# A selective scan on VectorE, with half of its C product handed to GpSimd and one intermediate kept in PSUM

## The reference, cut to what matters

```python
A = -jnp.exp(A_log)
dA = jnp.exp(jnp.einsum('bld,dn->bldn', dt, A))
dBx = jnp.einsum('bld,bln,bld->bldn', dt, B, x)

def step(h, inp):
    dA_t, dBx_t, C_t = inp
    h = dA_t * h + dBx_t
    y_t = jnp.einsum('bdn,bn->bd', h, C_t)
    return (h, y_t)
...
return y + x * D
```

## Time and profile before

| | us |
|---|---|
| Median of 3 runs (lowest, highest) | 1213.88 (1211.88, 1214.82) |
| Profiled execution, its own time | 1216.69 |
| Its span in the profile | 1214.9 |
| From the first B product (340.29) to the end of the last accumulation (495.90) | 155.61 |

### The profile page before, as it was taken

One profiled execution on the slowest core, in us unless ns is written; L12 is line 12 of the kernel. 1 busy time (PEld: TensorE's weight loads), 2 busy tenths in 40 slices (PEclk: granted clock), 3 DMA queues, 4 the chain that ended last, 5 costly groups with the idle time before them and its releaser, 6 DMA issues.

```text
span 1214.9 us, 15485 instructions
## 1 busy us (share of the span) xinstructions
PE 1015.3 (84%) x5192; PEld 644.1 (53%) x5202; DVE 836.2 (69%) x1392; ACT 619.5 (51%) x1493; POOL 494.6 (41%) x374
## 2 busy tenths in 40 slices
PE   5999879464646666358899999999999999999998
PEld 3777654223212222136667677777767565555554
DVE  4568639977699999767888877778787445332232
ACT  2445646066477663157778777687766223211111
POOL 0022277151056671137777765677654422100000
PEclk9878859778768787679999999999999999999999
DMA  9501130300100000000000014200003000000000
GB/s 334 243 1 51 69 139 0 125 32 5 24 0 1 0 0 0 2 1 1 2 1 2 1 45 126 70 2 1 2 1 122 1 1 1 1 18 1 1 1 18
DMA packets 24319, 43.78 MB, mean 36 GB/s; under 512 B 3616, under 2 KB 19936, under 8 KB 22624
## 3 DMA queue, kind: packets, MB, share of 16 engines
q1 hardware_dynamic: 24240, 42.79, 10.5%
HBM read 41.74 MB, written 1.05 MB: 35 GB/s over the span
## 4 chain that ended last, share of the span: by engine, by line
PE 58%; DVE 24%; ACT 10%; issue 5%; POOL 1%; DMA 1%; SPq 0%; DVEq 0%; ACTq 0%; POOLq 0%
PE ps L2165 12%; PE ps L2186 8%; DVE arena L982 6%; PE ps L1723 4%; PE ps L1736 4%; PE ps L1682 3%; DVE arena L978 3%; ACT arena L1027 3%; ACT ps L2011 3%; PE ps L1707 3%; PE ps L1690 3%; PE ps L437 2%; PE ps L400 2%; PE ps L1715 2%; PE ps L1697 2%
## 5 line engine op out<-in xcount | busy, mean ns | idle before, releaser
L2204 DVE TENSOR_TENSOR arena<-arena,ps 128x512 f32<-128x512 f32 (+1 forms) x56 | 38.5, 687 | 146.0 <-ACT arena L2197 143.9
L2089 POOL TENSOR_TENSOR arena<-arena 128x4 f32<-128x4 f32 x96 | 99.0, 1032 | 47.3 <-DVE arena L1839 44.5
L2197 ACT ACTIVATE arena<-ps,arena 128x512 f32<-128x512 f32 (+1 forms) x56 | 38.4, 686 | 156.0 <-PE ps L2165 156.0
L1061 PE MATMUL ps<-arena,ident 128*128 128x512 f32 x128 | 82.6, 781 | 37.6 <-DVE arena L987 37.6
L2186 PE MATMUL ps<-wide,arena 128*128 128x256 f32 (+1 forms) x448 | 106.3, 380 | 0.0
L2011 ACT ACTIVATE ps<-ps,arena 128x128 f32<-128x128 f32 x256 | 88.4, 355 | 28.3 <-DVE arena L1818 28.3
L2003 ACT ACTIVATE arena<-ps,arena 128x512 f32<-128x512 f32 x96 | 68.1, 784 | 65.9 <-PE ps L1697 65.8
L2186 PEld LDWEIGHTS ps<-wide,arena 128*128 128x128 f32 (+1 forms) x448 | 84.7, 190 | 17.9 <-issue 1.8
L2165 PE MATMUL ps<-XT,wide 128*128 128x512 f16 (+1 forms) x384 | 93.3, 379 | 0.0
L1818 DVE TENSOR_REDUCE arena<-ps 128x4 f32<-128x512 f32 x64 | 43.8, 690 | 47.5 <-PE ps L1707 47.4
L1690 PE MATMUL ps<-wide,arena 128*128 128x512 f16 x256 | 66.6, 397 | 11.2 <-POOL arena L2069 9.1
(11 more groups left out here) (322 smaller groups left out, 2469.1 us busy)
## 6 DMA issues: line engine op xcount, KB each, us to landing
side<-in_wproj SPq DMA_DIRECT2D x1, 4096.0 KB, 14.2
wide<-in_w_down SPq DMA_DIRECT2D x1, 3584.0 KB, 13.9
side<-in_w_gate SPq DMA_DIRECT2D x1, 3520.0 KB, 30.8
side<-in_w_up SPq DMA_DIRECT2D x1, 3520.0 KB, 12.1
wide<-in_w_gate SPq DMA_DIRECT2D x2, 1728.0 KB, 11.9
side<-in_w_up SPq DMA_DIRECT2D x3, 1024.0 KB, 9.3
arena<-in_taps SPq DMA_DIRECT2D x1, 2048.0 KB, 13.6
wide<-in_wq SPq DMA_DIRECT2D x1, 2048.0 KB, 10.7
```

Of the source, the lines that this page charges most:

```text
L1061: last = pe.matmul(ps[:, 4 + 2 * c + j, :], k.ident[:, :], read[i % 2][:, 512 * j:512 * j + 512], start=(n == 0), stop=(n == NST - 1), ski ...
L2089: pool.tensor_tensor(rs[:, j, :], var[:, j, :], minus_half[:, j, :], ALU.pow).then_inc(rs_ready, 1)
```

## The change

The two halves are treated differently. For the upper half (c = 1) the B product is written back over B in PSUM banks 0 and 1, and the scan reads it there. The SBUF space of the second `dBx` buffer becomes `c_copy`. ACT copies C from PSUM into it once per pair, and POOL makes the C product of the lower half (c = 0) from `state[0]` and `c_copy`. DVE makes only the C product of the upper half. The waits follow: `read_ready` is split in two; B of the next n is spread only after the upper scan (it reads bank 0), C only after ACT's copy and DVE's C product. Three semaphores elsewhere are merged or dropped.

```diff
-    dBx = [A.take([N]) for _ in range(2)]
+    dBx, c_copy = A.take([N]), A.take([N])
...
@@ vector
             wait(dve, state_ready, i - 1)
-            dve.tensor_tensor(dBx[i % 2], dtx[:, c, :], banks(0), ALU.mult).then_inc(dBx_ready, 1)
+            product = banks(0) if c else dBx
+            dve.tensor_tensor(product, dtx[:, c, :], banks(0), ALU.mult).then_inc(dBx_ready, 1)
             dve.wait_ge(dBx_ready, i + 1)
             dve.wait_ge(dA_ready, i + 1)
-            wait(dve, read_ready, i - 1)
-            dve.tensor_tensor_scan(state[i % 2], dA[i % 2], dBx[i % 2], 0.0, ALU.mult,
-                                   ALU.add).then_inc(state_ready, 1)
-            dve.wait_ge(state_ready, i + 1)
-            dve.wait_ge(c_psum, n + 1)
-            wait(dve, summed, i - 1)
-            dve.tensor_tensor(read[i % 2], state[i % 2], banks(2), ALU.mult).then_inc(read_ready, 1)
+            wait(dve, read1_ready if c else read0_ready, n)
+            dve.tensor_tensor_scan(state[c], dA[c], product, 0.0, ALU.mult, ALU.add).then_inc(state_ready, 1)
+            if c:
+                dve.wait_ge(state_ready, i + 1)
+                dve.wait_ge(c_taken, n + 1)
+                wait(dve, summed, i - 1)
+                dve.tensor_tensor(read[1], state[1], banks(2), ALU.mult).then_inc(read1_ready, 1)
@@ scalar, at the end of each step, behind split_scalar
+            if c:
+                act.wait_ge(c_psum, n + 1)
+                wait(act, read0_ready, n)
+                act.copy(c_copy, banks(2)).then_inc(c_taken, 1)
@@ tensor, accumulate(i)
-            pe.wait_ge(read_ready, i + 1)
+            pe.wait_ge(read1_ready if c else read0_ready, n + 1)
@@ tensor, the loop (spread no longer waits itself)
             accumulate(2 * n)
             if n + 1 < NST:
-                spread(n + 1, b_parts, 0, b_psum, dBx_ready)
-                spread(n + 1, c_parts, 2, c_psum, read_ready)
+                pe.wait_ge(state_ready, 2 * n + 2)
+                spread(n + 1, b_parts, 0, b_psum)
+                pe.wait_ge(read1_ready, n + 1)
+                pe.wait_ge(c_taken, n + 1)
+                spread(n + 1, c_parts, 2, c_psum)
             accumulate(2 * n + 1)
@@ gpsimd
-        for i in range(len(w.chunks)):
-            w.split_pool(pool, i, unsplit[i % 2])
+        for i, (n, c) in enumerate(STEPS):
+            if i < len(w.chunks):
+                w.split_pool(pool, i, unsplit[i % 2])
+            if c == 0:
+                pool.wait_ge(c_taken, n + 1)
+                pool.wait_ge(state_ready, i + 1)
+                wait(pool, summed, i - 1)
+                pool.tensor_tensor(read[0], state[0], c_copy, ALU.mult).then_inc(read0_ready, 1)
```

More of the change, by code:

```diff
@@ L920, in scan @@
     state_ready = k.sem("sc_state_ready")
-    read_ready = k.sem("sc_read_ready")
+    c_taken = k.sem("sc_c_taken")
+    read0_ready = k.sem("sc_read0_ready")
+    read1_ready = k.sem("sc_read1_ready")
     summed = k.sem("sc_summed")
@@ L1048, in tensor, with spread @@
             last.then_inc(dt_psum, 1)
-        def spread(n, rows, bank, done, free):
-            wait(pe, free, KC * n)
+        def spread(n, rows, bank, done):
             for j in range(2):
@@ L1066, in tensor @@
         pe.wait_ge(parts_ready, 1)
-        spread(0, b_parts, 0, b_psum, dBx_ready)
+        spread(0, b_parts, 0, b_psum)
         pe.wait_ge(parts_ready, 2)
@@ L1070, in tensor @@
         pe.wait_ge(dt_relu, 2)
-        spread(0, c_parts, 2, c_psum, read_ready)
+        spread(0, c_parts, 2, c_psum)
         for n in range(NST):
@@ L1391, in load_whole @@
         sp.dma_start(self.k.side[:, 0:KC * FM].rearrange("p (c n) -> p c n", c=KC),
-                     self.k.a["w_up1" if up else "w_gate1"].rearrange("(c p) n -> p c n", p=P)).then_inc(self.whole_loaded, 16)
+                     self.k.a["w_up1" if up else "w_gate1"].rearrange("(c p) n -> p c n", p=P)).then_inc(self.gate_loaded, 16)
     def square(self, act, i):
-        act.wait_ge(self.whole_loaded, 16 * (i // 4 + 1))
+        act.wait_ge(self.gate_loaded, 16 * (i // 4 + 1))
         wait(act, self.squared, i)
@@ L1411, in scale @@
         if v == 0:
-            dve.wait_ge(self.gate_loaded, 80)
+            dve.wait_ge(self.gate_loaded, 32 + 80)
         if v == 5:
@@ L1598, in cross @@
     lnT_psum = k.sem("xa_lnT_psum")
-    x_scales = k.sem("xa_x_scales")
     var_done = k.sem("xa_var_done")
@@ L1624, in cross @@
     w_used = k.sem("xa_w_used")
-    out_psum = k.sem("xa_out_psum")
     added = k.sem("xa_added")
@@ L1805, in vector @@
         dve.tensor_tensor(x_w, in_inv, ln_w.unsqueeze(2).broadcast_to([P, KC, 4]), ALU.mult)
-        dve.tensor_tensor(x_b, in_inv, ln_b.unsqueeze(2).broadcast_to([P, KC, 4]), ALU.mult).then_inc(x_scales, 1)
+        dve.tensor_tensor(x_b, in_inv, ln_b.unsqueeze(2).broadcast_to([P, KC, 4]), ALU.mult).then_inc(consts, 1)
         def quantise_x(b):
@@ L2019, in take_pT @@
             act.copy(flat(pT[t]), ps[:, 4 + t, :]).then_inc(pT_ready, 1)
-        act.wait_ge(x_scales, 1)
+        act.wait_ge(consts, 1)
         take_x(0)
-        act.wait_ge(consts, 1)
+        act.wait_ge(consts, 2)
         k.norm_scalar(act, 7, range(1, B))
@@ L2095, in gpsimd @@
         round_x(0)
-        pool.wait_ge(consts, 1)
+        pool.wait_ge(consts, 2)
         for j in range(3):
```

1 line of the change is left out of this document (removed).

## The result

The changed kernel takes 1223.02 us in the median of 4 runs (1221.21 to 1224.87), the one before 1214.12 (1211.88 to 1214.82). The ratio is 1.0069, with a 95% interval of 1.0044 to 1.0095: slower by about 8.9 us (5.3 to 11.5 by the interval), where 5.9 were forecast. The profiled execution took 1221.21. Further down, one of the ten runs of e4_warm (1284.89 us) and one of the six of e8_spread (3378.49 us) fell in a slower state, and the ratios leave them out.

The account below looks back on a forecast made before the run. Before, DVE bound at 9.42 us a pair (141.3); after, POOL and PE: 12 x 10.12 + 3 x 8.94 = 148.3, +7.0 less 1.1 = +5.9, on the median 1213.88 giving 1219.8 us, range 1205 to 1227.

Parts of the forecast that it names:

- DVE: One of two C products leaves DVE: 1.14 us less per pair, 8.28 a pair, 18.2 us if nothing else bound.
- POOL's product: POOL's C product of 1024 columns takes 2.36 us, between bounds of 2.12 and 2.56.
- in-place product: DVE's upper B product written into PSUM costs nothing extra; upper bound twice 1.21, costing 2.7 us in all.
- scan from PSUM: The upper scan's input from PSUM adds no time.
- Loop 1: Lower scan, POOL's product and two subtractions exclude each other at the SBUF port: 8.94 us a pair, upper scan exempt.
- Loop 2: Lower scan, POOL's product, PE's accumulation and B's spread, DVE's B product: 8.46 us a pair at high clock, 10.12 at low.
- How often the clock is low: PE's lower accumulation starts at the low clock in 12 of 15 intervals, after longer idle stretches.
- The end: Behind the last lower scan one C product is gone: -1.14 us.
- ACT's copy, the merged semaphores, the start: ACT's 1.01 us copy is hidden, merged semaphores add no wait, and the first pair starts as before.
- The clock up all through: Rival: PE's part is 2.42 us in nearly all pairs, loop 1 binds, -8.3 us, 1205.6; chance 0.13.
- DVE binding alone: Rival: neither port nor PE chain matters, -18.2 us, 1195.7; chance 0.02.
- The port taken by the upper scan as well: Rival: 11.23 us a pair, +26.0, 1239.9 us; chance 0.10 together with the clock low all through.

Follow-up runs that it names:

- e4_warm: Changed kernel plus 12 matmuls of zeros ahead of each lower accumulation but the first; 1218.22 us, ratio 1.0026 to the kernel before.
- e8_spread: Changed kernel with both spreads ahead of the lower accumulation and 26 chunks of side work laid evenly over 32 steps; 1203.08 us, ratio 0.9892 to before.
- e2_inplace: Kernel before with only the upper B product in place in PSUM and scanned there, DVE making both C products; 1214.78 us, ratio 0.9997 to before.
- e7_warm2: Changed kernel plus 8 matmuls of zeros in PE's idle stretch and 9 under POOL's product, per pair; 1204.78 us, ratio 0.9908 to before.
- e9_two_reads: Changed kernel with both spreads ahead of the lower accumulation and two buffers in turn for POOL's product; 1202.16 us, ratio 0.9891 to before.
- e3_pool: Changed kernel without the PSUM part, the upper B product going into a second SBUF buffer; 1232.56 us, ratio 1.0129 to before.
- e5_order_nosplit: Changed kernel with both spreads ahead of the lower accumulation and POOL's subtraction replaced by a memset; 1195.62 us, ratio 0.9826 to before.
- e1_order: Changed kernel with PE's list reordered, both spreads of the next n ahead of the lower accumulation; 1203.59 us, ratio 0.9898 to before.
- e6_nosplit: Changed kernel, PE's order as in the change, with POOL's subtraction replaced by a memset; 1226.82 us, ratio 1.0091 to before.

## Why the prediction was right, by its own steps

**DVE.** 16 x 1.14 = 18.2 was forecast to leave DVE; its busy time fell by 18.0. Right, and shown reachable: with the new order and the port free the intervals are 8.15 (forecast 8.28; the upper B product no longer waits for a C product of the same scan and starts 0.08 before the lower scan's row ends).

**POOL's product, in-place product, scan from PSUM.** 2.36 forecast, 2.356 measured; no surcharge for the PSUM operands forecast, 1205 and 2286 ns measured, and e2_inplace gives the whole part as 9.42 a pair, unchanged.

**Loop 1, the port.** 8.94 forecast; 8.83 measured wherever it binds (e7_warm2, e9_two_reads, the one high-clock interval after). The difference is in the borders: POOL's next instruction starts before the last one's row ends (404.94 to 407.02 is 2.08, for a row of 2.14), and a held scan ends 2.14 after the release. That the upper scan leaves the port alone was taken from a product's row and from the Trainium skill's page "SBUF — State Buffer", section "Who interferes with whom"; e2_inplace shows it for a scan (2.12 against 3.27), and e3_pool what it is worth. One sentence of the prediction was too wide: that a scan with two SBUF inputs and a POOL instruction never run together. It holds for the subtraction and the product; POOL's memsets ran beside such scans (in e5_order_nosplit from 348.98 to 350.81, beside the scan of 349.16), and these took 2.29.

**Loop 2, through POOL and PE.** 10.12 forecast, 10.24 measured, of which 0.13 and not 0.05 goes to POOL's start, and 4.15 and not 4.12 to PE and the handover. That this loop and not the port makes the pair is shown from three sides: take it away (e1_order), and the loss becomes a gain; speed up PE alone (e7_warm2), and the same; take the port away (e6_nosplit), and the settled pair stays at 10.24. The high-clock price of the loop, 8.46, is borne out by the last intervals of e7_warm2, 8.54.

**How often the clock is low.** This is the term that was mis-sized most. 12 of 15 intervals were taken as low; in the profile 14 were, the first and the last ten in full and three with parts of their matmuls at the high level (9.52 to 10.07). The intervals sum to 151.4 in place of 148.3. Of these 3.2 us more (151.44 against 148.26), 1.35 come from the second to fifth interval (38.29 in place of 10.12 + 3 x 8.94 = 36.94), 1.2 from the 0.12 more in each of the ten settled ones, and 0.65 from the first, where B's spread was slow too. The end gave 1.3 back (7.9 us from the last lower scan to the last accumulation, 9.2 before) where 1.1 was forecast. 10.1 - 1.3 = 8.8, which is the growth of the stretch, close to the 8.9 between the medians. The page "TensorE: Matmul & The Clock Gate" of the Trainium skill, section "What's actually happening", had been weighed at +9.4 us with all 15 low; the measurement came nearer to it than to the 12. What the prediction did not have was a way to tell which level an accumulation gets. It argued from the length of the idle stretch ahead, with one row behind 2.38 us that ran at 0.50. The kernel before has another behind the same 2.38 us that ran at 1.00:

```profile
365.47 1.98 PE L1061 MATMUL ps<-arena,ident 128*128 128x512 f32 x4 [2.38 <-DVE arena L987]
```

```profile
365.50:367.80 2.30, 2.30 (x6) 0.84 (x6) 2.27 (x2) 1.92 (x2) 0.87 (x2) 1.00 0.00 0
```

In the changed kernel the fifth pair's accumulation ran at 1.00 behind 3.26 us. So the 12 was a guess between 9 and 15, and that it came as near as it did is in part luck.

**ACT's copy, the merged semaphores, the start.** Forecast at nothing, and nothing was seen of them. ACT's copy starts 7.1 us behind the lower scan (409.62 against 402.49) and is through at 410.63, 2.2 before POOL starts on it.

**The rivals.** Each is set against the kernel before on the same chip. The clock up all through was priced at -8.3 us; e7_warm2, where it is up from the second pair on, takes 11.5 less than before (its intervals 7.7 less). DVE binding alone was priced at -18.2; e5_order_nosplit takes 20.6 less (intervals 16.3), but it also leaves POOL's subtractions out of the whole stage, so that its 1195.6 us meet the rival's 1195.7 is luck. The port taken by the upper scan as well was priced at +26.0; e3_pool, where it is, takes 17.0 more (intervals 19.2), because held instructions need less than their full length and pairs without subtractions are shorter.

## What to carry to other kernels

Work that is moved to a slower engine also moves its consumer: before giving a product away, follow who waits for it and what stands behind that wait in an in-order list. Here an accumulation that nobody needed soon stood ahead of a spread that everybody needed, and swapping the two lines of PE's order turned +0.7% into -1.0%. And if a matmul on the path starts behind an idle stretch, price it at each of the two levels of the clock and not at the mean: here the pair was 8.83 at the one and 10.24 at the other, and no row told beforehand which it would be.

## What the runs showed of the hardware that was not expected

- In the kernels where loop 2 binds, the pair settles at one length to within 0.01 us, 10.23 to 10.25, whatever POOL does beside it (after from the sixth interval on, e4_warm from the tenth, e6_nosplit from the fourth), and the clock falls and rises at the same place of every pair: in after all ten accumulations take 3.67 or 3.68 and the spreads behind them 1.03. Before it had settled, the second interval and those behind it were anything from 8.54 to 10.07. Why just this length was not tested.
- 12 matmuls in an idle stretch of 4 us, leaving 0.9 to 1.7 of it, kept the clock at 1.00 in some pairs and not in others; 17, leaving at most 0.4, kept it in all.
- A POOL memset runs beside a scan with two SBUF inputs without holding it up, at 0.95 us for 1024 f16 columns; but the very first product behind one started 4.3 us (e6_nosplit) and 3.8 us (e5_order_nosplit) after its last wait had ended. Behind a subtraction it takes 0.15 us (after, 343.35 against a scan end of 343.20), and later products behind memsets take 0.14 as well (e6_nosplit, 406.74 against 406.60). The cause is open.
